# Folded keys and values of a cross-attention computed on array tiles, in a decoder layer on one NeuronCore

## The reference, cut to what matters

```python
def xattn(x, context, mask, Wq, Wkv, Wout, b_out):      # x 16x512x256, context 16x64x256
    q = x @ Wq.T                                         # 1024 = 16 heads x 64
    k, v = jnp.split(context @ Wkv.T, 2, axis=-1)
    ...
    sim = jnp.einsum('bhid,bhjd->bhij', q, k) * SCALE
    sim = jnp.where(mask[:, None, None, :], sim, max_neg)
    attn = jax.nn.softmax(sim, axis=-1)
    out = jnp.einsum('bhij,bhjd->bhid', attn, v)
    return out @ Wout.T + b_out

x = _layernorm(x + attn_ref(x, ...))                     # linear attention, state 16x16 per head
x = _layernorm(x + xattn_ref(x, ctx_1024, mask, ...))
x = _layernorm(x + ffn_ref(x, ...))
```

## Time and profile before

| what | value |
|---|---|
| median of 3 runs | 1261.22 (1259.86 to 1261.81) |
| the profiled execution's own time | 1261.79 |
| its span | 1260.1 |
| setup up to the first scores | 0 to 104.5 |
| attention, 16 batches | about 104.5 to 870 |
| feed-forward | from about 870 to the end |
| busy PE, DVE, ACT, POOL | 97%, 69%, 45%, 50% |
| granted clock of TensorE, mean | 0.997 |

### The profile page before, as it was taken

One profiled execution on the slowest core, in us unless ns is written; L12 is line 12 of the kernel. 1 busy time (PEld: TensorE's weight loads), 2 busy tenths in 40 slices (PEclk: granted clock), 3 DMA queues, 4 the chain that ended last, 5 costly groups with the idle time before them and its releaser, 6 DMA issues.

```text
span 1260.1 us, 24107 instructions
## 1 busy us (share of the span) xinstructions
PE 1219.2 (97%) x8848; PEld 1100.2 (87%) x8848; DVE 868.0 (69%) x1694; ACT 567.2 (45%) x1117; POOL 623.7 (50%) x986
## 2 busy tenths in 40 slices
PE   8979999999999999999999999988999999999998
PEld 7868889898898898988988989887798899899888
DVE  5557888888888888888888888887533323322435
ACT  2144556555546465556465655555423312421420
POOL 3245766766756767567567575665322112202201
...
DMA packets 117912, 69.88 MB, mean 55 GB/s; under 512 B 74658, under 2 KB 115363, under 8 KB 117796
## 3 DMA queue, kind: packets, MB, share of 16 engines
...
q10 hardware_dynamic: 2032, 0.66, 0.2%
...
## 4 chain that ended last, share of the span: by engine, by line
PE 79%; DVE 9%; issue 2%; POOL 1%; ACT 1%; POOLq 0%; DVEq 0%
PE ob L137 7%; PE ob L138 6%; PE ob L139 6%; PE sim L137 6%; PE sim L138 6%; PE sim L139 6%; PE pw L440 4%; PE pw L137 3%; PE pw L138 3%; PE pw L139 3%; PE pt L489 3%; PE pw L390 3%; PE pt L139 2%; PE pt L138 2%; PE pt L137 2%; DVE prob L848 2%
## 5 line engine op out<-in xcount | busy, mean ns | idle before, releaser
L1595 POOL TENSOR_TENSOR w_lo<-w_raw,w_hi 128x2048 fp32r<-128x2048 f32 x16 | 73.7, 4609 | 222.5 <-ACT w_hi L1535 169.3
L137 PE MATMUL ob<-b_hi,pT_hi 128*128 128x256 f32 x512 | 153.3, 299 | 14.6 <-DVE pT_lo L855 14.6
L138 PE MATMUL ob<-b_lo,pT_hi 128*128 128x256 f32 x512 | 144.5, 282 | 0.0
L139 PE MATMUL ob<-b_hi,pT_lo 128*128 128x256 f32 x512 | 144.2, 282 | 0.0
L950 POOL TENSOR_TENSOR prob<-prob,rz 128x512 f32<-128x512 f32 x128 | 130.9, 1044 | 10.4 <-DVE rz L796 10.4
L711 ACT ACTIVATE prob<-prob 128x512 f32<-128x512 f32 x128 | 80.8, 631 | 112.0 <-DVE prob L848 111.4
L843 DVE TENSOR_REDUCE mx<-sim 128x8 f32<-128x512 f32 x128 | 88.2, 689 | 40.1 <-PE sim L139 39.1
L137 PEld LDWEIGHTS ob<-b_hi,pT_hi 128*128 128x128 f32 x512 | 97.5, 190 | 19.4 <-DVE pT_lo L855 18.7
L137 PE MATMUL sim<-a_hi,tT_hi 128*128 128x512 f32 x256 | 103.9, 406 | 0.0
L623 ACT ACTIVATE x<-h,nmr,rstd 128x256 f32<-128x256 f32 x128 | 76.3, 596 | 58.5 <-POOL nmr L869 53.7
L138 PE MATMUL sim<-a_lo,tT_hi 128*128 128x512 f32 x256 | 101.3, 396 | 0.0
...
## 6 DMA issues: line engine op xcount, KB each, us to landing
...
```

The lines of the kernel that those rows point to most:

```text
L137: pe.matmul(out, lh, rh, start=first, stop=False)
L138: pe.matmul(out, lh, rl, start=False, stop=False)
L139: return pe.matmul(out, ll, rh, start=False, stop=last)
```

## The change

A and B are computed on parts of the array. The keys and values lie as 64 rows (channels of a head) by 64 columns, one half of the heads on partitions 0 to 63 and the other on 64 to 127, without zeros. Two preparations are now one piece of PE's program (`TOGETHER`): A0 with A2, A1 with A3, B0 with B1, B2 with B3, each of the two in its own bank. A pair of A is 16 float32 matmuls of 64 rows by 128 columns with 64 moving columns, in turn on the upper and the lower 64 rows of the array. A pair of B is 8 float32 matmuls of 64 rows by 64 columns with 256 moving columns, in turn on the four quarters of the array, in place of 12 of `three_passes`. The splits of the values and of Wout go (`v_hi`, `v_lo`, `wox_hi`, `wox_lo`). A has two buffers, for even and odd batches, `vraw` too. The tables of places are new, DVE has a place 10 at the end of a slot and a place 1, ACT a place 7, and in slots 2 and 3 DVE does `pT_lo` of half 1 ahead of `tT_lo`. In the setup the loads of Wkv, Wq and Wout come in halves or quarters so that the heads land where they are wanted.

```diff
     ORDER = {
-        "G": ((0, 4), (0, 8), (0, 8)), "B0": ((0, 7), (0, 8), (1, 0)),
-        "B1": ((0, 7), (1, 0), (1, 0)), "GT": ((1, 1), (1, 3), (1, 3)),
-        "B2": ((1, 3), (1, 5), (1, 8)), "B3": ((1, 5), (1, 6), (1, 9)),
-        "T1": ((1, 7), (1, 8), (1, 9)), "T0": ((1, 7), (1, 9), (2, 0)),
-        "R": ((1, 7), (2, 0), (2, 9)), "ST": ((2, 5), (2, 7), (3, 0)),
-        "A1": ((3, 1), (3, 0), (3, 2)), "A0": ((3, 1), (3, 1), (3, 3)),
...
+        "G": ((0, 4), (0, 7), (0, 8)), "GT": ((0, 5), (0, 7), (0, 8)),
+        "B0": ((0, 7), (0, 8), (1, 0)), "B1": ((0, 7), (0, 8), (1, 0)),
+        "B2": ((1, 1), (1, 1), (1, 3)), "B3": ((1, 1), (1, 1), (1, 3)),
+        "T1": ((1, 5), (1, 8), (1, 10)), "T0": ((1, 7), (1, 9), (2, 0)),
+        "R": ((1, 8), (2, 0), (2, 9)),
+        "A0": ((2, 2), (2, 3), (2, 5)), "A2": ((2, 2), (2, 3), (2, 5)),
+        "A1": ((2, 7), (2, 8), (2, 10)), "A3": ((2, 7), (2, 8), (2, 10)),
+        "ST": ((2, 8), (2, 8), (3, 1)),
+        "SB": ((3, 7), (3, 8), (3, 10)), "SW": ((3, 7), (3, 8), (3, 10)),
...
+    TOGETHER = {"A0": "A2", "A1": "A3", "B0": "B1", "B2": "B3"}
...
         elif name[0] == "A":
-            need(pe, "k_loaded", 32 * (b + 1))
-            m, hf = i % 2, i // 2
-            for r in range(PAIRS // 2):
-                pr = hf * (PAIRS // 2) + r
-                c = slice(m * P, (m + 1) * P)
-                last = pe.matmul(pw[:, r * P:(r + 1) * P], wqx[:, pr, c], kraw[:, pr, :], start=True, stop=True)
+            need(pe, "k_loaded", 16 * (b + 1))
+            c = slice(i * P, (i + 1) * P)
+            for r in range(PAIRS):
+                for g, mate in enumerate(mates):
+                    d = slice(g * NKV, (g + 1) * NKV)
+                    last = pe.matmul(pws[bank_of(mate)][:, r * NKV:(r + 1) * NKV], wqx[d, r, c], kraw[d, r, :],
+                                     start=True, stop=True)
+                    if r == PAIRS - 1 and g == 0:
+                        last.then_inc(s["prep_made"], 1)
         else:
-            need(pe, "v_hi_made", b + 1)
-            need(pe, "v_lo_made", b + 1)
+            need(pe, "v_loaded", 16 * (b + 1))
             for r in range(2):
-                pr = 2 * i + r
-                last = three_passes(pe, pw[:, r * C:(r + 1) * C], (v_hi[:, pr, :], v_lo[:, pr, :]),
-                                    (wox_hi[:, pr, :], wox_lo[:, pr, :]), True, True)
+                for g, mate in enumerate(mates):
+                    for o in range(2):
+                        d, keys, h = slice(g * NKV, (g + 1) * NKV), slice(o * NKV, (o + 1) * NKV), 2 * (i + r) + o
+                        last = pe.matmul(pws[bank_of(mate)][keys, r * C:(r + 1) * C], vraw[d, q, h, :], wox[d, h, :],
+                                         start=True, stop=True)
...
+        pT_first = slot >= 2 and it < NB - 1
+        if has_prev and pT_first:
+            dve_pT(dve, n - 1, 1)
...
-        if slot == 3 and within(it + 1):
-            need(pool, "v_hi_made", it + 2)
-            pool.tensor_tensor(v_lo[:, :, :], vraw[:, :, :], f32(v_hi[:, :, :]), ALU.subtract).then_inc(s["v_lo_made"], 1)
...
-        pool.memset(kraw[:, :, :], 0.0)
-        pool.memset(vraw[:, :, :], 0.0)
```

More of the change, by code:

```diff
@@ L361, in x_tiles @@
         return t["x"][bass.ds(b, 1), :, :].rearrange("o (i p) c -> p (o i) c", p=P)
-    def load_kv(sp, dst, which, b, sem):
-        for h in range(2):
-            q = slice(64 * h, 64 * h + 64)
-            if isinstance(b, int):
-                src = kv_scr[which, b, q, :, :]
-            else:
-                src = kv_scr[which, bass.ds(b, 1), q, :, :].rearrange("o p r j -> (o p) r j")
-            sp.dma_start(dst[q, :, 64 * h:64 * h + 64], src).then_inc(s[sem], 16)
     def pe_prep(pe, name, it, q):
+        if name in TOGETHER.values():
+            return
         b = batch_of(name, it)
         pw = pws[bank_of(name)]
+        mates = (name, TOGETHER[name]) if name in TOGETHER else (name,)
         latest = {}
-        for back, other in [before_on_bank(it, name)] + [(0, x) for x in OPERANDS.get(name, ())]:
+        for back, other in [before_on_bank(it, x) for x in mates] + [(0, x) for x in OPERANDS.get(name, ())]:
             if other:
@@ L542, in pe_slot @@
         n = 4 * it + slot
-        prep = lambda place: [pe_prep(pe, x, j, par(0)) for x, j in at("pe", slot, place, it)]
+        prep = lambda place: [pe_prep(pe, x, j, par(it - j)) for x, j in at("pe", slot, place, it)]
         if has_sim:
@@ L660, in act_slot @@
         prep(1)
-        if slot == 3 and within(it + 1):
-            need(act, "v_loaded", 32 * (it + 2))
-            if within(it):
-                need(act, "prep_made", number(it, last_of("B0", "B1", "B2", "B3")))
-            act.activation(v_hi[:, :, :], vraw[:, :, :], ACT.Copy).then_inc(s["v_hi_made"], 1)
         if has_sim:
@@ L776, in dve_slot @@
             dve_stats(dve, 2, n - 2, q, h2[:, q, :])
+        prep(1)
         if has_sim:
@@ L812, in dve_slot @@
             ff["dve_up"](dve, 0, tail_tile(it, slot))
-        if has_prev:
+        if has_prev and not pT_first:
             dve_pT(dve, n - 1, 1)
+        prep(10)
         if (it, slot) == (NB - 1, 0):
-            need(dve, "v_lo_made", NB)
             ff["dve_free"](dve)
@@ L1010, in setup_and_attention @@
     x1 = k.sb("x1", [P, 2, TPB, C + 1])
[L1011 to L1012 removed]
+    a_odd = [k.sb(f"a_{part}", [P, MC, KEYS], F32R) for part in ("hi", "lo")]
     b_lo = k.sb("b_lo", [P, PAIRS, C], F32R)
[L1014 to L1015 removed]
+    vraw = k.sb("vraw", [P, 2, PAIRS, NKV])
+    k.sb("w2_hi1_room", [P, PAIRS, P])
+    a_even_hi = k.sb_over("hT_lo1_room", "a_even_hi", [P, MC, KEYS])
+    a_hi = ([a_even_hi[:, m, :] for m in range(MC)], [a_odd[0][:, m, :] for m in range(MC)])
+    a_lo = ([k.sb_over(room, f"a_even_lo{m}", [P, KEYS])[:, :] for m, room in enumerate(("x2T_lo_room", "w2_hi1_room"))],
+            [a_odd[1][:, m, :] for m in range(MC)])
     prob = k.sb("prob", [P, 2, KEYS])
@@ L1218, in _ @@
                 if n == 6:
-                    sp.dma_start(wqx[:, :, 1:C + 1], t["L0_xattn_Wq"].rearrange("(i p) c -> p i c", p=P)).then_inc(loaded["wqx"], 16)
+                    for half in range(2):
+                        sp.dma_start(wqx[half * NKV:(half + 1) * NKV, :, 1:C + 1], wq_halves[half]).then_inc(loaded["wqx"], 16)
                 if n == 8:
@@ L1225, in _ @@
                 if n == 14:
-                    sp.dma_start(wout_raw[:, :, :], t["L0_xattn_Wout"].rearrange("(m p) n -> p m n", p=P)).then_inc(loaded["wout"], 16)
+                    for m in range(MC):
+                        for quarter in range(4):
+                            a, half = quarter // 2, quarter % 2
+                            cols = slice(quarter * C, (quarter + 1) * C)
+                            sp.dma_start(wout_raw[:, m, a * W:(a + 1) * W].rearrange("p (i g d) -> p g i d", g=2, d=NKV)[:, half],
+                                         t["L0_xattn_Wout"][m * P:(m + 1) * P, cols].rearrange("p (i d) -> p i d", d=NKV)
+                                         ).then_inc(loaded["wout"], 16)
             if u == PREPS[4]:
```

82 lines of the change are left out of this document (44 added, 38 removed), and 13 rows, old and new, of tables (FIRST_ORDER, ORDER).

## The result

The changed kernel takes **1298.7 us** (median of 4 runs, 1296.6 to 1299.4) against 1261.5 before (4 runs on the same chip): a ratio of **1.029, with a 95% interval of 1.028 to 1.031**. It is 37 us slower, where I had forecast 10 (1271 us), and lies just over the end of my range. Its profiled execution has a span of 1297.7 us, against 1260.1 before. One of the four executions of e1, further down, took 4234 us and is left out of its figures.

A forecast was written before the change was run, and what follows sets the result against it. PE's work in order bounds the kernel, with DVE close behind. A batch was to take 51.15 us against 50.25, +12.6 over fourteen, less 3 in the start: 1271 us from 1261.8, range 1240 to 1298.

The forecast's parts named there:

- The A pair: On PE, 32 records paced by loads side by side, 56 ns each: 2.0 us a pair, 0.2 more than before.
- The B pair: On PE, 16 records running four side by side, plus changes of shape: 1.08 us a pair, 0.34 less than before.
- Rivals 3, 4 and 5: B's quarters two at a time, 1296, 0.10; A's halves load one after the other, 1322, 0.08; no overlap, some 1395, 0.02.
- Rival 1: A pairs on PE: loads hide and the halves stream side by side, a pair 1.1 us, total 1246 us; chance 0.20.
- Slots 2 and 3: 13.6 and 13.3 us: the 0.93 wait goes, PE waits 0.65 and 1.3 at pt of half 1 for pT_lo.
- Rival 2: DVE catches up in slots 2 and 3, so the two waits of 1.95 together don't arise: 1244 us; chance 0.16.
- the term of GT: Slot 0: GT, now ahead of pt of half 1, waits for ACT's copies of G behind tT_hi: 0.15 us more.
- The setup and iteration -1: Before the steady batches: less work and fewer waits between A quarters, between -4 and +1 us, taken as -3.
- the clock is no term: TensorE's granted clock stays at the full 2.4 GHz through a steady batch, so it adds nothing to the forecast.

The follow-up runs named there:

- e1: Changed kernel with ST ahead of the A pairs in iteration -1 alone: 1297.3 us, ratio 1.029 to the kernel before.
- e4: Changed kernel with each A matmul cut in two along its output columns, so a pair runs on four quarters of the array: 1269.6 us, ratio 1.006.
- e3: Changed kernel with the splits of A0 and A2 moved behind pT of half 0 on ACT and DVE: 1289.0 us.
- e6: Changed kernel with GT moved in slot 0 from ahead of pt of half 1 to behind it: 1292.5 us.
- e13: Changed kernel with matmuls nobody reads added in iteration -1, ahead of each A pair and SB: 1293.9 us, ratio 1.026.
- e10: Changed kernel with e4, e6, e8's start, ST's sum and POOL's state sum later in slot 3, A0 with A2 between pt's halves: 1244.2 us, ratio 0.987.
- e2: Changed kernel with Wkv, Wq and Wout loaded in plain order by the 6 DMAs of before instead of 18: 1296.4 us, ratio 1.027.
- e8: Changed kernel with e1, e3, e4, e6, ST's sum on DVE behind pT_lo, and A0 with A2 in slot 1 of iteration -1: 1333.3 us.

## Why the prediction was half right

**The pairs: right.** The A pair is 2.02 us with both changes of shape (forecast 2.0): its records come two per 112 ns, as two loads of 128 columns side by side would have it. e4 is the proof. With loads of 64 columns on four tiles, four records come in 58 to 60 ns and the pair is 1.18. The B pair is 1.12 (1.08): four records 7 ns apart, then the next four 216 ns after the first. Rivals 3, 4 and 5 are out. Rival 1 lacks its premise, since the loads don't hide. In sum the tiles give PE nothing. With both changes of shape, the two pairs of A cost 4.04 us where the four quarters took 3.40, and the two pairs of B 2.23 where they took 2.84.

By the Trainium skill, TensorE: Matmul & The Clock Gate, section "Measured speedup vs the span model", a group of tiles takes one matmul and some 4 ns a tile. The trace agrees nearly for B (216 ns for four records of 256 columns, their starts 6 to 7 ns apart) and for A on quarters (60 ns for four of 64), and not for A on halves (112 ns for two of 64): the rule has no term for a load that is longer than the stream beside it.

**Slots 2 and 3: right.** 27.1 us against 26.9, the 0.93 ahead of the second product gone, a wait at `pt` of half 1 in each slot, both released by `pT_lo`. I had 0.65 and 1.3, it is 0.78 and 1.09, so two small errors partly cancel in the sum. Rival 2 (DVE catches up) is out: DVE idles ahead of A's splits, where I said it would. That this order on DVE makes the wait in slot 2 is shown by e3.

**Slot 0: the term of GT was mis-sized.** I gave it 0.15 for the wait and nothing for itself. The wait is 0.54 (e6 removes it), and GT's own 0.14 us is there too (in slot 1 it had taken 0.11). With these and the B pair, 12.05 - 1.42 + 1.12 + 0.54 + 0.14 = 12.43, of 12.53 measured. The error was to count ACT's `tT_hi` alone as standing ahead of the copies of G. ACT works without a gap there, and two norms stand ahead of `tT_hi` (537.48 and 537.97 us, half a microsecond each; `tT_hi` at 538.47, the copies at 538.94 and 539.31). It is most of the 0.83 us a batch by which I was low, and with it of 12 us.

**The setup and iteration -1: the step that failed.** "The setup and iteration -1 lose the split of Wout, the zeroing, and part of the waits between A quarters", -3: it is +14.6. The error is 17.6 us, the largest. I counted the work that went and not the order of what stayed. Three things came in its place:

- *The order and the pairs.* ST and then SB, over DVE and POOL, is a chain of 6 to 7 us. Before, three quarters of A lay beside it. In the changed kernel both pairs come first, and nothing lies beside it. Putting ST first (e1) doesn't help much, since a pair needs both banks: 2.4 us.
- *The clock.* Behind these gaps TensorE falls to its lower level, and both pairs of A, ST and much of what follows up to the first scores go at half pace. I had written that the clock is no term, and it isn't in a steady batch. From the first T1 to the first scores it takes 19.8 us before (84.72 to 104.52), 30.0 after (89.07 to 119.10), and 24.3 in e13 (87.74 to 112.04). So of 10.2 us more, 5.7 are the clock and 4.5 the waits themselves, by these three executions.
- *The 4.4 us ahead of T1*: 1.35 in the setup, the rest in iteration -1, where G's 16 records took 3.6 us at the low clock instead of 2.8 in this execution, and in e4, e6 and e10 did not. In 14 profiles with the changed setup the first `zb` lies between 77.2 and 79.9 us, against 75.88 in the single one of before; e2 shows that the pieces of the weights are not why. Where these 1 to 4 us come from stays open.

Quarters and the new start (e8) bring the stretch from `zb` to the first scores from 41.9 to 32.3 us; before it was 28.6.

So the direction stands, and the mechanism of slots 2 and 3, down to where PE waits and for what; the size failed, by a start that I had not walked through and a wait on ACT's order in slot 0.
